# GpSimd takes the low parts of LoRA B, and the third unit runs P7 before P3 with c22 ahead of the tile turns

## The chip, the cores and the metric

The kernel runs on one core of one Trainium2 chip. The metric is the device time of one execution in microseconds. Its engines are TensorE (PE, with its weight loads as PEld), VectorE (DVE), ScalarE (ACT), GpSimd (POOL) and SyncE (SP); each runs its own list of instructions in order, and they wait for one another on semaphores.

## The reference

Two residual layers over 2048 tokens of width 1024 (x has shape 8 x 256 x 1024), all in float32:

```
gate = x @ W_gate.T + 0.5 * (x @ A_gate[i].T) @ B_gate[i].T     # F = 2752, rank 16
up   = x @ W_up.T   + 0.5 * (x @ A_up[i].T)   @ B_up[i].T
act  = silu(gate) * up
x    = x + act @ W_down.T + 0.5 * (act @ A_down[i].T) @ B_down[i].T
x    = x + x @ W.T + bias + scale[j] * (x @ a[j].T) @ b[j].T     # i, j: adapter of the batch entry
```

## The kernel before

Float32 products are made of three matmuls on rounded halves: every operand is split into a high part (a copy rounded to fp32r, made by ScalarE) and a low part (the value less its high part, a subtraction), and high x high, high x low and low x high are summed in PSUM. The tokens are worked through in two halves of 1024. In each half the 2752 rows of gate and up are worked through in 22 units of 128 rows (the last has 64). `U` counts units over both halves (0 to 43), `u` within a half (0 to 21). After both halves come a down stage and an out stage, which the change doesn't touch.

A unit computes a 2 x 2 block of products: gate and up (the two rows) times two chunks of 512 tokens (the two columns): c11, c12 (gate), c21, c22 (up). Units 0 and 1 of a half do this plainly. From unit 2 on, a scheme with seven products in place of eight is used. Its stages are P1 to P7, each of 12 matmuls of 128x512, in an order of its own: P1 P6 P5 P7 P2 D P4 P3 in ordinary units, and in the third unit (u = 2, `PLAIN`) P1 P6 P5 P2 D P3 P7 P4, since some of its inputs are made last. D is one adapter matmul alone; P2, P3 and P4 end in one adapter matmul each. The stages use these weights: P1 A11, P6 S2, P5 S1, P7 S3, P2 A12, P4 A22, P3 S4. A11 to A22 are parts of the turned gate and up tiles (`TG`, `TU`), S1 to S4 sums of them, made by VectorE: s1 = a21 + a22, s2 = s1 - a11, s3 = a11 - a21, s4 = a12 - s2. On the side of the tokens, P1 uses B11, P2 B21, P3 B22, P4 T4, P5 T1, P6 T2, P7 T3, where the T are sums of the x blocks, and T3 and T4 of a half are made and split during units 1 and 2. P3 and P4 are added in PSUM onto earlier contents of their bank, which VectorE must have read before: P3 goes to the bank of P5 (waits for `v_done`), P4 to the bank of P7 (waits for `c22_done`) in the third unit; in ordinary units P4 goes to the bank of P7 and waits for `v_done`, P3 to that of P5 and waits for `c22_done`.

The high and low parts of the weights go through a ring of four slots, in the order of the stages: ScalarE's `w_high` waits until the stage that used the slot four items earlier has ended, then makes the high part; GpSimd's `w_low` (L1839) waits for it and makes the low part; TensorE waits for the low part.

What VectorE does in an ordinary unit, in order: `second_act` of the unit before, `add_q` (L662, after P6), `turn_tile` of G and U of the next unit (L514, which waits for the low parts of A12 and A22 of this unit), in odd units `turn_b`, sums 1 to 3 of the next unit, in eight units of each half (`SPILL_UNITS`, u = 3 to 6 and 9 to 12) a turn of an x block for the spill (`("y", h, n)`, L579), `add_v` (L668 and L670; the first makes `v_done`, both `c22_done`), sum 4, `add_c22` (after D), `b_low`, `first_act` (L695, L698), `add_c12` (L703). In the third unit (`third_unit`): `add_q`, `x_low` of T3, sum 3, `add_v_third` (L677), `x_low` of T4 twice (L614), the turns of G and U, sums 1 and 2, `add_c22_third` (L683, which makes `c22_done`), `add_c22`, sums 3 and 4, `b_low`, `first_act`, `add_c12`.

The adapters: x times LoRA A of a half is in `Tm` (for gate and up), split high and low and stacked over the partitions in bands of 32; `Bf[u % 2]` holds LoRA B in bands that fit: three bands with the high part, one with the low part, for gate (w = 0) and up (w = 1). `ts` holds turned B for two units (`turn_b`, L635). ScalarE's `b_high(U)` (L1471) makes six copies of 32x256, then VectorE's `b_low(U)` (L648) two subtractions of 32x256. An adapter matmul of unit U waits for `bf_lo` at U + 1:

```
            def adapter(U, w, p, dst, start=False):
                h = U // UNITS
                eng.wait_ge(bf_lo, U + 1)
                eng.wait_ge(t_lo, 4 * h + 2 * p + w + 1)
```

In unit 0 of a half `Tm` is only made, so the adapters of unit 0 (E11, E21, E12, E22) run in unit 1, and right behind them E11 and E21 of unit 1 itself. ScalarE makes `b_high` of unit 0, then T1, `Tm`, then `b_high` of unit 1. Every matmul has line L1954 in the profile; operands tell the stages apart: `X_B` are blocks B11, B21, B22, `X_T` are T1, T2, T4 and T3 (also B12, which shares T3's place), `Tm_g,Bf` and `Tm_u,Bf` are adapters.

Of the kernel before, what the change touches and what calls it, by code (L numbers as in the profile page):

```python
# [5 lines left out]
F32 = mybir.dt.float32  # L6
# [32 lines left out]
def build(nc, x, l0_index, l1_index, w_gate, w_up, w_down, a_gate, b_gate, a_up, b_up, a_down, b_down,  # L39
# [19 lines left out]
    with ExitStack() as ctx:  # L59
# [148 lines left out]
        def stages_of(u):  # L208
# [4 lines left out]
            if u == PLAIN:  # L213
                return ["P1", "P6", "P5", "P2", "D", "P3", "P7", "P4"]
# [223 lines left out]
        def b_places(u, w, source, to, also):  # L438

            src = ts[source, :].rearrange("p (r f) -> p r f", r=2)  # L440
            homes = [Bf[u % 2][rows, w, :, :] for rows in (to, also)]
            if u < FULL - 1:
                src = src.rearrange("p r (q c i) -> p r q c i", q=NQ, c=2)[:, :, :, u % 2, :]
                homes = [home.rearrange("p r (q i) -> p r q i", q=NQ) for home in homes]
            elif u == FULL - 1:
                src = src[:, :, 0:P]
            else:
                src, homes = src[:, :, P:P + HC], [home[:, :, w * HC:(w + 1) * HC] for home in homes]
            return src, homes[0], homes[1]
# [30 lines left out]
        def _(eng):  # L480
# [160 lines left out]
            def b_low(U):  # L641
                u = U % UNITS
                eng.wait_ge(bf_hi, U + 1)
                for w in range(2):
                    rows = slice(w * Q, (w + 1) * Q)
                    lo = slice(BF_LO[w] * Q, (BF_LO[w] + 1) * Q)
                    src, dst, hi = b_places(u, w, rows, lo, rows)
                    last = V.tensor_tensor(dst, src, hi.bitcast(F32), ALU.subtract)  # L648
                last.then_inc(bf_lo, 1)

# [90 lines left out]
            def first_unit(U):  # L741
# [19 lines left out]
                b_low(U)  # L761
# [4 lines left out]
                b_low(U + 1)  # L766
# [3 lines left out]
            def second_unit(U):  # L770
# [36 lines left out]
            def unit(U):  # L807
# [19 lines left out]
                b_low(U + 1)  # L827
# [529 lines left out]
        def _(eng):  # L1357
# [102 lines left out]
            def b_high(U):  # L1460
                u = U % UNITS
                eng.wait_ge(b_turned, U // UNITS * BLOCKS + u // 2 + 1)
                if U >= 2:
                    wait_stage(eng, *last_stage(U - 2))
                for w in range(2):
                    if u == FULL:
                        A.activation(Bf[u % 2][:, w, :, (1 - w) * HC:(2 - w) * HC], zeros[:, :, :], ACT.Copy)
                    for r in BF_HI[w]:
                        rows = slice(r * Q, (r + 1) * Q)
                        src, home, _ = b_places(u, w, slice(w * Q, (w + 1) * Q), rows, rows)  # L1470
# [51 lines left out]
            def second_unit(U):  # L1522
# [8 lines left out]
                silu_plain(U)  # L1531
                b_high(U + 1)
                w_high(U + 1, "S1")
# [4 lines left out]
            def third_unit(U):  # L1538
                h = U // UNITS
                copy_p1(U)  # L1540
                w_high(U, "S4")
# [3 lines left out]
                w_high(U, "S3")  # L1545
# [267 lines left out]
        def _(eng):  # L1813
# [37 lines left out]
            def first_unit(U):  # L1851
# [12 lines left out]
                for item in ("A11", "A12", "A21", "A22"):  # L1864
                    w_low(U + 1, item)

            def second_unit(U):
                for item in ("A11", "S2", "S1", "A12"):
                    w_low(U + 1, item)

            def third_unit(U):
                for item in ("S4", "S3", "A22"):
                    w_low(U, item)
                for item in ("A11", "S2", "S1", "S3"):
                    w_low(U + 1, item)
# [25 lines left out]
            for U in range(ALL):  # L1901
# [49 lines left out]
        def _(eng):  # L1951
# [160 lines left out]
            def third_unit(U):  # L2112
# [11 lines left out]
                up(U, "D", adapter(U, 1, 1, d, start=True))  # L2124
                eng.wait_ge(v_done, seven_half(U))
# [268 lines left out]
```

## Time and profile before

| | |
|---|---|
| time, median of 3 runs | 1652.75 us (1651.93 to 1652.83) |
| the profiled execution | 1652.34 us, span 1650.3 us |
| mean granted clock of TensorE | 0.998 |
| TensorE busy | 1615.0 us, 98% |
| VectorE, ScalarE, GpSimd busy | 1129.6, 535.8, 653.8 us (68, 32, 40%) |
| the chain that ended last, by engine | 85% TensorE, 5% VectorE |

The span is the time from the first to the last instruction of the core. TensorE is almost never idle, so its few idle stretches and its granted clock are what a change of order can reach. A matmul's printed duration covers its way through the pipeline, so single ones overlap: read the distance from start to start.

### The profile page before, as it was taken

To read this page: it belongs to the slowest core of one execution; us is meant where nothing else is said; L and a number is where in the kernel's file an instruction comes from. 1 tells how busy PE (TensorE), PEld (TensorE's weight loads), DVE (VectorE), ACT (ScalarE), POOL (GpSimd) and SP (SyncE) were. 2 spreads that over 40 slices of the span, in tenths; PEclk is the share of its full clock that TensorE was granted. 3 is DMA by queue.
4 is the path that set the end of the run, shared out by engine and by line. 5 is a ranking of instruction groups with operands and counts; after the bars stand their busy time and mean duration, and the time that the engine had idled before them with its cause. 6 is when DMAs were issued, how large, how long until landed. Compare 5 with 4: busy or idle time off the path is not lost.

```text
span 1650.3 us, 21023 instructions
## 1 busy us (share of the span) xinstructions
PE 1615.0 (98%) x7060; PEld 1314.0 (80%) x7060; DVE 1129.6 (68%) x1286; ACT 535.8 (32%) x925; POOL 653.8 (40%) x441
## 2 busy tenths in 40 slices
PE   6999999999999899999999999999999999999998
PEld 4778888888887788888888788888888887778886
DVE  5887777777768877777776665566665578856433
ACT  3744444444446444444444221111111121431110
POOL 5254444444452444444444452323332331541110
PEclk9999999999999999999999999999999999999999
DMA  8334434423433344344334742122222131013322
GB/s 158 104 91 109 144 93 106 150 80 96 120 101 91 93 105 144 98 112 146 81 80 128 275 124 67 45 77 80 80 55 77 62 70 28 18 29 80 79 52 53
DMA packets 218125, 156.12 MB, mean 95 GB/s; under 512 B 110692, under 2 KB 200164, under 8 KB 215268
## 3 DMA queue, kind: packets, MB, share of 16 engines
q1 hardware_dynamic: 169536, 114.92, 27.3%
q10 hardware_dynamic: 48356, 39.86, 7.7%
q8 instruction: 58, 0.95, 0.2%
q14 instruction: 47, 0.39, 0.1%
q0 software_dynamic: 128, 0.00, 0.0%
HBM read 115.38 MB, written 39.32 MB: 94 GB/s over the span
## 4 chain that ended last, share of the span: by engine, by line
PE 85%; DVE 5%; SPq 4%; issue 2%; ACT 2%; POOL 1%; DMA 1%; DVEq 0%; ACTq 0%
PE ps L1954 85%; SPq L463 1%; SPq L1207 1%; DVE X_T L614 1%; SPq L1199 1%; ACT Bf L1471 1%; SPq L1171 1%; DVE TU L514 0%; DVE TG L514 0%; POOL W L1839 0%; SPq L1224 0%; DMA raw<-in_L_cond_W_up_dram 0%; DMA act_scratch<-vbuf 0%; DVE s L547 0%; DVE s L540 0%
## 5 line engine op out<-in xcount | busy, mean ns | idle before, releaser
L1954 PE MATMUL ps<-X_T,W 128*128 128x512 f32 x1944 | 460.4, 392 | 11.8 <-DVE vbuf L683 5.2
L1954 PE MATMUL ps<-act,Wd 128*128 128x512 f32 x2016 | 462.4, 390 | 1.4 <-POOL Wd L1888 1.4
L1954 PEld LDWEIGHTS ps<-act,Wd 128*128 128x128 f32 x2016 | 378.6, 188 | 81.5 <-POOL Wd L1888 1.8
L1954 PEld LDWEIGHTS ps<-X_T,W 128*128 128x128 f32 x1944 | 364.7, 188 | 94.2 <-DVE vbuf L668 7.6
L1954 PE MATMUL ps<-X_B,W 128*128 128x512 f32 x1728 | 417.7, 392 | 14.0 <-ACT X_B L1416 13.3
L1954 PEld LDWEIGHTS ps<-X_B,W 128*128 128x128 f32 x1728 | 325.6, 189 | 83.9 <-issue 15.5
L940 DVE TENSOR_TENSOR acc<-acc,ps 128x1024 f32<-128x1024 f32 x176 | 214.1, 1220 | 176.1 <-PE ps L1954 175.6
L1839 POOL TENSOR_TENSOR W<-s,W 128x512 fp32r<-128x512 f32 x156 | 210.8, 1351 | 256.3 <-ACT W L1387 256.3
L1839 POOL TENSOR_TENSOR W<-TG,W 128x512 fp32r<-128x512 f32 x88 | 129.8, 1476 | 175.8 <-ACT W L1387 175.7
L1387 ACT ACTIVATE W<-s 128x512 fp32r<-128x512 f32 x156 | 98.4, 632 | 239.2 <-PE ps L1954 232.7
L1880 POOL TENSOR_TENSOR act<-stage,act 128x1024 fp32r<-128x1024 f32 x42 | 100.6, 2414 | 173.7 <-ACT act L1623 173.7
L1954 PE MATMUL ps<-X1hi,Wo 128*128 128x512 f32 x512 | 141.4, 390 | 0.0
L1954 PEld LDWEIGHTS ps<-X1hi,Wo 128*128 128x128 f32 x512 | 96.2, 188 | 20.4
L1471 ACT ACTIVATE Bf<-ts 32x256 fp32r<-32x256 f32 (+1 forms) x264 | 107.9, 409 | 8.7 <-DVE ts L635 6.1
L1623 ACT ACTIVATE act<-stage 128x1024 fp32r<-128x1024 f32 x42 | 42.4, 1048 | 184.7 <-PE ps L1954 164.8
L662 DVE TENSOR_TENSOR qbuf<-p1buf,ps 128x512 f32<-128x512 f32 x38 | 26.1, 687 | 100.1 <-PE ps L1954 100.0
L1888 POOL TENSOR_TENSOR Wd<-turned,Wd 128x512 fp32r<-128x512 f32 x44 | 55.8, 1291 | 74.0 <-ACT Wd L1657 74.0
L1387 ACT ACTIVATE W<-TG 128x512 fp32r<-128x512 f32 x88 | 55.3, 629 | 91.3 <-PE ps L1954 84.1
L1839 POOL TENSOR_TENSOR W<-TU,W 128x512 fp32r<-128x512 f32 x46 | 65.7, 1431 | 39.4 <-ACT W L1387 39.4
L1954 PE MATMUL ps<-X1lo,Wo 128*128 128x512 f32 x256 | 80.3, 390 | 0.0
L1888 POOL TENSOR_TENSOR Wo<-turned,Wo 128x512 fp32r<-128x512 f32 x16 | 21.7, 1378 | 124.4 <-ACT Wo L1657 124.4
L698 DVE TENSOR_TENSOR c21buf<-c21buf,s1buf 128x512 f32<-128x512 f32 x38 | 67.9, 1787 | 1.3
(134 smaller groups left out, 1512.2 us busy)
## 6 DMA issues: line engine op xcount, KB each, us to landing
stage<-act_scratch SPq DMA_DIRECT2D x21, 1024.0 KB, 5.0
raw<-in_L_cond_W_gate_dram SPq DMA_DIRECT2D x164, 128.0 KB, 3.0
raw<-in_L_cond_W_up_dram SPq DMA_DIRECT2D x164, 128.0 KB, 3.1
raw<-in_x_dram SPq DMA_DIRECT2D x104, 128.0 KB, 3.1
raw<-in_L_cond_W_down_dram SPq DMA_DIRECT2D x88, 128.0 KB, 3.2
act_scratch<-c21buf ACTq DMA_DIRECT2D x42, 256.0 KB, 2.4
act_scratch<-vbuf ACTq DMA_DIRECT2D x42, 256.0 KB, 2.8
xt_scratch<-xt ACTq DMA_DIRECT2D x4, 2048.0 KB, 7.0
```

The lines of the kernel that those rows point to most:

```text
L463: eng.dma_start(buf[q * Q + b * R:q * Q + (b + 1) * R, w * HQ:(w + 1) * HQ], rows[:, q * HQ:(q + 1) * HQ]).then_inc(filled, 16)
L614: V.tensor_tensor(x_home(name, kq, 1), x_source(name, kq), x_home(name, kq, 0).bitcast(F32), ALU.subtract).then_inc(x_lo_d.up((h, name, kq ...
L662: V.tensor_tensor(qbuf[:, :], p1buf[:, :], bank(U % 2, "b"), ALU.add).then_inc(q_done, 1)
L698: V.tensor_tensor(c21buf[:, :], c21buf[:, :], s1buf[:, :], ALU.mult).then_inc(act1_done, 1)
L940: V.tensor_tensor(acc[pr][:, k, :], acc[pr][:, k, :], src[:, :], ALU.add).then_inc(b_added.up(s), 1)
L1387: A.activation(hi, src, ACT.Copy).then_inc(w_hi, 1)
L1471: last = A.activation(home, src, ACT.Copy)
L1623: A.activation(acts[t % 3][:, 0, cols], stage[t % 2][:, cols], ACT.Copy).then_inc(act_hi.up((t, pr)), 1)
L1839: G.tensor_tensor(low, src, hi.bitcast(F32), ALU.subtract).then_inc(w_lo, 1)
L1880: G.tensor_tensor(acts[t % 3][:, 1, cols], stage[t % 2][:, cols], acts[t % 3][:, 0, cols].bitcast(F32), ALU.subtract).then_inc(act_lo.up(( ...
L1888: last = G.tensor_tensor(low, src, hi.bitcast(F32), ALU.subtract)
L1954: return nc.tensor.matmul(dst, stationary, moving, start=start, stop=stop, skip_group_check=True)
```

## The change

Three edits at once. (1) In the third unit P7 moves ahead of P3. S3 and S4 change places in all queues: VectorE makes sum 3 during unit 1 and sum 4 in the third unit. `add_c22_third` and `add_c22` move ahead of the turns and sums of the next unit. On ScalarE S1's high part of the third unit moves ahead of `b_high`. (2) The low parts of LoRA B move from VectorE to GpSimd (`b_low`), placed behind A11's low part of the next unit in most units. ScalarE makes one more copy per unit, a rounded copy of both bands into `b_round`, from which GpSimd subtracts; the bands of `Bf` are arranged so that the low part stands in the band of its source. `b_high` waits until the previous `b_low` has read `b_round`. (3) In the eight spill units `add_v` comes ahead of the turn of the x block.

```diff
-                return ["P1", "P6", "P5", "P2", "D", "P3", "P7", "P4"]
+                return ["P1", "P6", "P5", "P2", "D", "P7", "P3", "P4"]
...
-        TM_LO = (slice(2 * Q, 3 * Q), slice(Q, 2 * Q))
-        TM_AGAIN = (slice(3 * Q, 4 * Q), slice(0, Q))
-        BF_HI = ((0, 1, 2), (1, 2, 3))
-        BF_LO = (3, 0)
+        TM_LO = (slice(2 * Q, 3 * Q), slice(0, Q))
+        TM_AGAIN = (slice(3 * Q, 4 * Q), slice(Q, 2 * Q))
+        BF_HI = ((1, 2, 3), (0, 2, 3))
+        b_round = at("b_round", 209664, [2 * Q, 256], F32R)
...
 VectorE: b_low(U) and every call of it removed
 VectorE, first_unit
                 x_sum(h, "T1", 1)
-                b_low(U)
                 x_low(h, "T2", 0)
...
-                b_low(U + 1)
                 x_low(h, "T1", 1)
 VectorE, second_unit
-                sums(U + 1, (4,))
+                sums(U + 1, (3,))
                 plain_act2(U)
-                b_low(U + 1)
                 x_low(h, "T3", 0)
 VectorE, third_unit
                 x_low(h, "T3", 1)
-                sums(U, (3,))
+                sums(U, (4,))
                 add_v_third(U)
                 x_low(h, "T4", 0)
                 x_low(h, "T4", 1)
+                add_c22_third(U)
+                add_c22(U)
                 turn_tile(("G", U + 1))
                 turn_tile(("U", U + 1))
                 sums(U + 1, (1, 2))
-                add_c22_third(U)
-                add_c22(U)
                 sums(U + 1, (3, 4))
-                b_low(U + 1)
 VectorE, unit
+                add_v(U)
                 if u in SPILL_UNITS:
                     turn_x(("y", h, SPILL_UNITS.index(u)))
-                add_v(U)
                 if u + 1 < FULL:
                     sums(U + 1, (4,))
                 add_c22(U)
-                b_low(U + 1)
 ScalarE, b_high
+                both = slice(0, 2 * Q)
+                if U >= 1:
+                    eng.wait_ge(bf_lo, U)
+                A.activation(b_rounded(u, both), b_places(u, 0, both, both)[0], ACT.Copy)
 ScalarE, second_unit
+                w_high(U + 1, "S1")
                 b_high(U + 1)
-                w_high(U + 1, "S1")
 ScalarE, third_unit
-                w_high(U, "S4")
+                w_high(U, "S3")
                 store_act(U - 1)
                 x_high(h, "T4", 0)
                 x_high(h, "T4", 1)
-                w_high(U, "S3")
+                w_high(U, "S4")
 GpSimd
+            def b_low(U):
+                u = U % UNITS
+                eng.wait_ge(bf_hi, U + 1)
+                eng.wait_ge(w_lo, made[0])
+                for w in range(2):
+                    rows = slice(w * Q, (w + 1) * Q)
+                    src, dst = b_places(u, w, rows, rows)
+                    last = G.tensor_tensor(dst, src, b_rounded(u, rows).bitcast(F32), ALU.subtract)
+                last.then_inc(bf_lo, 1)
+                eng.wait_ge(bf_lo, U + 1)
 GpSimd, first_unit: b_low(U) and b_low(U + 1) behind the four w_low of U + 1
 GpSimd, second_unit
+                w_low(U + 1, "A11")
+                w_low(U + 1, "S2")
+                w_low(U + 1, "S1")
+                b_low(U + 1)
+                w_low(U + 1, "A12")
 GpSimd, third_unit and ordinary units (there A12, A22, S4 first)
+                for item in ("S3", "S4", "A22"):
+                    w_low(U, item)
+                w_low(U + 1, "A11")
+                b_low(U + 1)
+                for item in ("S2", "S1", "S3"):
+                    w_low(U + 1, item)
 TensorE, third_unit
+                eng.wait_ge(q_done, seven_half(U))
+                up(U, "P7", stage_p(U, "P7", b))
                 eng.wait_ge(v_done, seven_half(U))
                 stage_p(U, "P3", c, start=False)
                 up(U, "P3", adapter(U, 0, 1, c))
-                eng.wait_ge(q_done, seven_half(U))
-                up(U, "P7", stage_p(U, "P7", b))
                 eng.wait_ge(c22_done, seven(U))
```

## Rows read from the trace of the kernel before

**Rows 1.** The page, its head and the busy time of the engines.

```profile
span 1650.3 us, 21023 instructions
...
PE 1615.0 (98%) x7060; PEld 1314.0 (80%) x7060; DVE 1129.6 (68%) x1286; ACT 535.8 (32%) x925; POOL 653.8 (40%) x441
```

**Rows 2.** Waits: who waited for whom: us in total, times, longest.

```profile
POOL W L1839 <- ACT W L1387: 471.5, 275, 14.9
...
PEld ps L1954 <- DVE vbuf L668: 7.6, 16, 2.2
...
PE ps L1954 <- DVE vbuf L683: 5.2, 2, 2.6
...
PE ps L1954 <- DVE vbuf L668: 2.2, 2, 1.8
```

**Rows 3.** Timeline of TensorE, units 2 and 3: start, length, [idle before].

```profile
72.26 2.88 PE L1954 MATMUL ps<-X_B,W 128*128 128x512 f32 x12
74.98 2.88 PE L1954 MATMUL ps<-X_T,W 128*128 128x512 f32 x12
78.96 3.00 PE L1954 MATMUL ps<-X_T,W 128*128 128x512 f32 x12 [1.10 <-issue]
...
93.99 4.56 PE L1954 MATMUL ps<-X_T,W 128*128 128x512 f32 x12 [2.57 <-DVE vbuf L683]
...
98.62 2.89 PE L1954 MATMUL ps<-X_B,W 128*128 128x512 f32 x12
...
112.75 3.02 PE L1954 MATMUL ps<-X_T,W 128*128 128x512 f32 x12
```

**Rows 4.** A window: busy time of each engine, then the granted clock.

```profile
93.99:95.00 1.01, 1.01 (x2) 0.83 (x3) 0.96 (x2) 0.59 (x2) 0.86 (x1) 0.50 0.13 35
```

**Rows 5.** Timeline of TensorE in half 1, units 24 and 25.

```profile
524.18 2.88 PE L1954 MATMUL ps<-X_B,W 128*128 128x512 f32 x12
...
531.34 3.01 PE L1954 MATMUL ps<-X_T,W 128*128 128x512 f32 x12 [1.55 <-POOL W L1839]
...
546.12 3.06 PE L1954 MATMUL ps<-X_T,W 128*128 128x512 f32 x12 [2.62 <-DVE vbuf L683]
...
549.24 2.88 PE L1954 MATMUL ps<-X_B,W 128*128 128x512 f32 x12
...
565.25 3.01 PE L1954 MATMUL ps<-X_T,W 128*128 128x512 f32 x12 [1.80 <-DVE vbuf L668]
```

**Rows 6.** Timeline of the other engines, units 2 and 3.

```profile
74.29 2.56 ACT L1471 ACTIVATE Bf<-ts 32x256 fp32r<-32x256 f32 x6 [3.06 <-DVE ts L635]
...
77.59 1.27 POOL L1839 TENSOR_TENSOR W<-s,W 128x512 fp32r<-128x512 f32 x1 [5.47 <-ACT W L1387]
...
85.28 3.44 DVE L614 TENSOR_TENSOR X_T<-xt,X_T 128x1024 fp32r<-128x1024 f32 x2
...
88.65 1.23 DVE L514 STREAM_TRANSPOSE TG<-raw 128x1024 f32<-128x1024 f32 x1
...
93.25 0.68 DVE L683 TENSOR_TENSOR vbuf<-vbuf,ps 128x512 f32<-128x512 f32 x1
...
105.10 1.25 DVE L514 STREAM_TRANSPOSE TG<-raw 128x1024 f32<-128x1024 f32 x1
```

**Rows 7.** Timeline around the first adapters, unit 1 of half 0.

```profile
56.68 2.56 ACT L1471 ACTIVATE Bf<-ts 32x256 fp32r<-32x256 f32 x6
...
59.27 0.85 DVE L648 TENSOR_TENSOR Bf<-ts,Bf 32x256 fp32r<-32x256 f32 x2 [1.90 <-ACT Bf L1471]
...
60.48 0.39 PE L1954 MATMUL ps<-Tm_g,Bf 128*128 128x512 f32 x1
```

**Rows 8.** Groups by line and form: busy, mean ns of one, idle before.

```profile
L1893 POOL TENSOR_TENSOR Ad<-Ad_turned,Ad 128x256 fp32r<-128x256 f32 x11 | 8.2, 747 | 51.0 <-ACT Ad L1680 51.0
```

**Rows 9.** Timeline of VectorE in unit 25, half 1.

```profile
556.89 1.25 DVE L514 STREAM_TRANSPOSE TG<-raw 128x1024 f32<-128x1024 f32 x1 [0.96 <-POOL W L1839]
```

**Rows 10.** The instructions of line L698: duration in ns, min/median/max.

```profile
L698 DVE TENSOR_TENSOR c21buf<-c21buf,s1buf x38: 691/1825/1830, 99.5 to 909.8; 128x512 f32<-128x512 f32 x38
```

More of the change, by code:

```diff
@@ L436, in item_places, with b_places @@
             return src[:, :].rearrange("p (k m) -> p k m", k=KT)[:, ks, :], wo[:, 0, ks, :], wo[:, 1, ks, :]
-        def b_places(u, w, source, to, also):
-            src = ts[source, :].rearrange("p (r f) -> p r f", r=2)
-            homes = [Bf[u % 2][rows, w, :, :] for rows in (to, also)]
+        def b_places(u, w, source, to):
+            src, home = ts[source, :].rearrange("p (r f) -> p r f", r=2), Bf[u % 2][to, w, :, :]
             if u < FULL - 1:
                 src = src.rearrange("p r (q c i) -> p r q c i", q=NQ, c=2)[:, :, :, u % 2, :]
-                homes = [home.rearrange("p r (q i) -> p r q i", q=NQ) for home in homes]
+                home = home.rearrange("p r (q i) -> p r q i", q=NQ)
             elif u == FULL - 1:
@@ L447, in b_places, with b_rounded @@
             else:
-                src, homes = src[:, :, P:P + HC], [home[:, :, w * HC:(w + 1) * HC] for home in homes]
-            return src, homes[0], homes[1]
+                src, home = src[:, :, P:P + HC], home[:, :, w * HC:(w + 1) * HC]
+            return src, home
+        def b_rounded(u, rows):
+            if u < FULL - 1:
+                return b_round[rows, :].rearrange("p (r q i) -> p r q i", r=2, q=NQ)
+            if u == FULL - 1:
+                return b_round[rows, :].rearrange("p (r f) -> p r f", r=2)
+            return b_round[rows, 0:2 * HC].rearrange("p (r f) -> p r f", r=2)
         def load_first(eng, kind, w):
@@ L639, in turn_b @@
                 last.then_inc(b_turned, 1)
[L641 to L649, printed above, removed]
             def t_low(h, p, w):
@@ L1865, in first_unit, with third_unit @@
                     w_low(U + 1, item)
+                b_low(U)
+                b_low(U + 1)
             def second_unit(U):
-                for item in ("A11", "S2", "S1", "A12"):
-                    w_low(U + 1, item)
[L1871 to L1875, printed above, removed]
+                w_low(U + 1, "A11")
[3 more added lines that the diff above has]
+                w_low(U + 1, "A12")
+            def third_unit(U):
+                for item in ("S3", "S4", "A22"):
+                    w_low(U, item)
+                w_low(U + 1, "A11")
+                b_low(U + 1)
+                for item in ("S2", "S1", "S3"):
+                    w_low(U + 1, item)
+            def b_low(U):
[8 more added lines that the diff above has]
+                eng.wait_ge(bf_lo, U + 1)
             def act_low(t, pr):
@@ L1911, in _ @@
                         w_low(U, item)
-                    for item in ("A11", "S2", "S1", "S3"):
+                    w_low(U + 1, "A11")
+                    b_low(U + 1)
+                    for item in ("S2", "S1", "S3"):
                         w_low(U + 1, item)
@@ L1916, in _ @@
                         w_low(U, item)
-                    for item in ("A11", "N", "A12", "S"):
+                    w_low(U + 1, "A11")
+                    b_low(U + 1)
+                    for item in ("N", "A12", "S"):
                         w_low(U + 1, item)
```

3 lines of the change are left out of this document (1 added, 2 removed).

## The prediction

> **What bounds the kernel now.** I read the page first. TensorE is busy for 1615.0 of 1650.3 us; no other engine comes to 70% [rows 1]. So only stretches in which TensorE stands still, or runs at the lower clock, can be won. The profiled execution took 1652.34 us, 2.04 more than its span and 0.41 under the median of 1652.75; the sum below is a difference, and I take it off the median.
>
> Next, the waits of TensorE [rows 2]. The start apart, the largest is 5.2 us in two pieces behind L683, the addition that makes c22 in the third unit of each half. Then comes L668, `v_done`: 2.2 us in two pieces, and, on the weight-load side, 16 waits with 7.6 us. There are 16 units that turn an x block ("y") for the spill.
>
> Then TensorE's timeline through the third unit (unit 2) of half 0 [rows 3]. One stage of 12 matmuls advances the start by 2.72 us (72.26 to 74.98) and one adapter matmul by 0.23. Seven stages and four adapters are 19.95. Unit 2 starts at 72.26 and unit 3 at 98.62, which is 26.36: 6.4 us are lost. P5 starts at 78.96 in place of 77.70, 1.26 late. P4 starts at 93.99 after 2.57 of idle, and its 12 matmuls last 4.56 in place of 2.88. The reader should see two costs in that one row: the wait, and 1.7 us because the granted clock is 0.50, so 1.2 GHz, right behind it [rows 4]. The other 0.9 are restarts and small waits. In half 1 [rows 5] the same unit takes 25.06 (524.18 to 549.24), 5.1 over, with no slow P4.
>
> Last, who is late in that unit [rows 6]. P5 waits for the low part of S1: ScalarE makes six Bf copies from 74.29 for 2.56 us, only then S1's high part, and GpSimd ends the low part at 78.86. P4 waits for c22: VectorE turns G and U of the next unit from 88.65 and makes two sums before L683 at 93.25.
>
> **The change, part by part.** *Order and turns of the third unit.* P7 goes ahead of P3, and both c22 additions ahead of the turns. P7 ends, P3 and its adapter run 2.95, and only then does P4 want c22. L683 needs 0.68 [rows 6] and each hand-over 0.1 to 0.3 (GpSimd ends at 78.86, P5 starts at 78.96), so it has about 2 us to spare. S3 and S4 change places in all queues with it: S3's sum is now made in the unit before, and S4's sum (once for once) is behind `add_q`. Does that hold? Unit 2 now starts at 73.46 (below), so P5 ends at 81.6 and VectorE has made `v_done` by about 83.1. Then the two low parts of T4 on VectorE and those of S4 and A22 on GpSimd take turns, as now (3.44 us for the first two [rows 6]): four of some 1.25, S4's there near 85.6 where P3 wants it at 87.5, A22's near 88.1 to 88.9 where P4 wants it at 90.5. So P4's wait goes, and with it its slow clock.
>
> *S1 ahead of `b_high`.* S1's high part no longer sits behind the Bf copies. Its ring slot frees when d1 of unit 1 ends, one stage and one adapter (2.95) before P1 of unit 2, so it is ready before P5. P5's wait goes. A12 is next behind the Bf copies. These become seven: 7 x 0.42 = 3.0 us. VectorE turns b some 2 us earlier, since unit 1 loses its last `b_low` and the wait in front of it, so they end at about 75.3; two x copies (2.0) and A12 follow, its low part is there near 79.5 to 80, and P2 wants it at 81.6. Covered. Both halves' third units therefore run at about 19.95: 6.4 + 5.1 = 11.5 us are removed, before what is added.
>
> *`b_low` on GpSimd.* It removes two VectorE operations per unit (0.42 each [rows 7]) and adds one ScalarE copy (0.42) and two GpSimd subtractions. No row has 32x256 on GpSimd. From below: VectorE's 0.42 each. From above: 1.27 for 128x512 [rows 6]. The nearest row is 128x256 at 0.75 [rows 8], the same elements in each partition, so I take 1.5 for the pair and keep 0.85 to 2.6.
> In ordinary units this is hidden. After P7 ends, ScalarE makes A11 and seven copies (0.2 + 0.6 + 3.0), GpSimd the pair and then S2's low part: about 0.5 + 1.5 + 1.3, so it is there after some 7.4 us. P6 of the next unit wants it 4 stages and 4 adapters later, 11.8 us. 4.4 are to spare. GpSimd idles 471.5 us behind ScalarE's high parts [rows 2].
> It isn't hidden at the adapters of unit 1. There ScalarE starts the copies of unit 1 at 56.68, ends them 2.56 later, VectorE's pair ends at 60.12, and TensorE takes that adapter at 60.48 without a wait [rows 7]. Now there is one more copy in each of `b_high(U)` and `b_high(U+1)`, 0.85 later: 60.1. The pair ends at 61.6, so E11 of unit 1 starts about 1.2 late. The same rows stand in half 1. Added: 2 x 1.2 = 2.4 us.
>
> *What is late next: unit 3.* The turns have not become cheaper, only later. With unit 1's loss, unit 2 starts at 73.46, P7 ends at 87.5 and unit 3 starts at 93.4. VectorE takes c22 at 87.75, and does then the work it did from 88.65 on. From the turn of G(3) to that of G(4) it was 16.45 us (88.65 to 105.10 [rows 6]), which hangs on the chain L703, silu, `copy_p1`, A12's high and low part. Less 0.85 for the moved `b_low`, and some 0.3 of a wait for P4 in it, it is 15.3. So G(4) is turned from 103.05, and from there to P4 of unit 3 it was 7.65 (105.10 to 112.75) in half 0 and 8.36 (556.89 to 565.25) in half 1 [rows 3, 5, 6, 9]. Without the x turn (1.2), that is now behind `add_v`, 6.45 and 7.2: P4 of unit 3 at 109.5 to 110.25. I take 110.0. Its ideal would be 107.5, so 2.5 us are given back. A second path says nearly the same: S2's low part now waits for `b_low`, which waits for seven copies behind G(3)'s turn; it comes at about 98, P6 wants it at 96.1.
> Before, P4 of unit 3 stood at 112.75: half 0 wins 2.75. In half 1 everything lies 451.92 later (524.18 less 72.26), P4 at 561.9 against 565.25: 3.35.
> GpSimd and VectorE are a cost in this. L698 with both inputs in SBUF takes 0.69 at least and 1.83 in most units [rows 10], there with a GpSimd operation under way. I count one such wait for S4's sum and one for L698. The Trainium skill (SBUF — State Buffer, section on the two separate sides) has a rule that speaks against moving `b_low` there: a VectorE operation with two SBUF inputs and a GpSimd operation lock each other out for a whole instruction. By the rule both waits stand; if the two ran side by side, each half would win about 0.7 more, 1.4 in all.
>
> *The x turn behind `add_v` in the other 14 spill units.* There P4 starts 0.06 late and lasts 0.14 longer (3.02 against 2.88, as at 112.75 [rows 3]): 0.2. One is 0.7 (idle 0.42, the smaller of the two in rows 2). VectorE's x turn takes as long as its other turns (1.23 to 1.25), and the lateness is less in each: 13 x 0.2 + 0.7 = 3.3 us won. Its raw slot frees 1.3 us later; the load that takes it is wanted in the next unit, some 15 us on.
>
> **Sum:** 2.75 + 3.35 + 3.3 = 9.4 us off: 1643.3 us. The down and out stages are untouched.
>
> **Rivals.** *Given back little.* If VectorE's chain is some 2 us shorter per half than I make it (fewer waits between it and GpSimd), unit 3 runs near its ideal: 4 to 5 us more, 1639. For it: the operations alone are shorter than in the trace. Against: the chain is the trace's own, measured.
> *The clock falls elsewhere.* Half 0's idle 2.57 brought 0.50 [rows 4]; half 1's 2.62, 1.55 and 1.80 did not (12 matmuls in 3.01 to 3.06 behind each [rows 5]). The new waits (E11, P6 and P4 of unit 3, each 1 to 2 us) could bring it in two places: 2 x 1.7, 1646.7. The Trainium skill (TensorE: Matmul & The Clock Gate, Part 1) says that idleness brings the lower clock and that it needs busy time to rise again; by that the new waits are suspects, and the rule gives no more than this rival has.
> *Given back whole.* G(4), and with it `v_done`, comes 2 to 3 us later per half (b copies, turn and A12 in an unlucky order), or the 14 small waits stay: 3 to 6 us less, 1647 to 1650; at its end no change that can be told.
> *Slower: the pair on GpSimd is long.* Each half pays for it twice, at E11 and in front of S2 or in the chain to G(4). With a pair of X us the loss is 4 (X - 1.5): nothing is won from X = 3.9, and it is slower by over 0.2% from X = 4.7, 2.35 us an operation. Beyond 5.9 the ordinary units' slack goes too, each of some 36 paying the rest. At X = 5.5: 16 lost, 1659. For it: strided reads of 32 partitions have no row. Against: 1.27 for twice the elements.
>
> **Chances and range.** A measurement can tell about 0.2%, 3.3 us, from no change: faster is under 1649.4. Forecast (1641 to 1646) 0.62; given back little 0.13; clock 0.09; given back whole 0.10, of which 0.06 within 0.2%; slower 0.05; the last 0.01 lies with no change. So faster 0.88, same 0.07, slower 0.05. The range leaves out the slow end and the luckiest: 1638.5 to 1648.
>
> **What would show it.** Right: P5 and P4 of the third units start without idle and P4 lasts 2.9; new idle of about 1.2 at the first `Tm_g,Bf` of unit 1 behind POOL Bf; P6 or P4 of unit 3 late by 2 to 3 in all; no weight-load waits behind L668 in units 4 and on; POOL Bf pairs of about 1.5, ScalarE Bf copies 7 a unit, POOL busy up by about 60 us. Wrong: P4 of the third units behind POOL W or X_T; a pair over 2.6; P6 waits in ordinary units; granted clock 0.50 behind E11 or in unit 3.

## The result, and the profile after

The changed kernel takes 1642.49 us (median of 5 runs, 1641.36 to 1645.11) against 1652.37 for the kernel before (median of 5 beside it, 1651.93 to 1652.83): ratio 0.9939 [0.9927, 0.9951], so 9.9 us faster. The forecast was 1643.3. The profiled execution took 1642.49 us, 1.69 more than its span. Unchanged code has new line numbers: L1971 is the matmul (L1954 before), L680 c22's addition in the third unit (L683), L665 `v_done` (L668), L1834 `w_low` (L1839), L521 and L586 the turns of weights and of x (L514, L579), L1466 the Bf copies (L1471). New are L1460, the rounded copy of `b_high`, and L1886, `b_low` on GpSimd.

The page of after, its head, the engines, and the group of the new pair (busy time, mean ns of one, idle before):

```profile
span 1640.8 us, 21154 instructions
...
PE 1609.4 (98%) x7060; PEld 1313.4 (80%) x7060; DVE 1069.9 (65%) x1198; ACT 554.2 (34%) x969; POOL 727.0 (44%) x529
...
L1886 POOL TENSOR_TENSOR Bf<-ts,b_round 32x256 fp32r<-32x256 f32 (+1 forms) x88 | 73.4, 834 | 64.7 <-ACT Bf L1466 45.7
```

Against [rows 1] VectorE has 59.7 us less, GpSimd 73.2 more, TensorE 5.6 less. The waits of TensorE in after (total, times, longest):

```profile
PE ps L1971 <- POOL W L1834: 3.8, 2, 1.9
PE ps L1971 <- POOL Bf L1886: 2.6, 2, 1.6
```

All of TensorE's waits that [rows 2] named are gone: the two pieces behind c22, the waits behind `v_done`, the 16 on the weight-load side. Two new pairs stand in their place. TensorE's timeline of after shows where (start, length, idle before): the first adapters of unit 1, then units 2 and 3 of half 0, then half 1.

```profile
60.30 0.39 PE L1971 MATMUL ps<-Tm_u,Bf 128*128 128x512 f32 x1
62.30 0.50 PE L1971 MATMUL ps<-Tm_g,Bf 128*128 128x512 f32 x1 [1.62 <-POOL Bf L1886]
...
74.22 2.88 PE L1971 MATMUL ps<-X_B,W 128*128 128x512 f32 x12
76.94 5.60 PE L1971 MATMUL ps<-X_T,W 128*128 128x512 f32 x24
...
94.17 2.88 PE L1971 MATMUL ps<-X_B,W 128*128 128x512 f32 x12
98.93 8.40 PE L1971 MATMUL ps<-X_T,W 128*128 128x512 f32 x36 [1.88 <-POOL W L1834]
...
110.35 1.98 PE L1971 MATMUL ps<-X_T,W 128*128 128x512 f32 x8
...
507.01 0.39 PE L1971 MATMUL ps<-Tm_g,Bf 128*128 128x512 f32 x1
...
509.03 0.50 PE L1971 MATMUL ps<-Tm_g,Bf 128*128 128x512 f32 x1 [0.94 <-POOL Bf L1886]
...
520.97 2.88 PE L1971 MATMUL ps<-X_B,W 128*128 128x512 f32 x12
...
540.91 2.88 PE L1971 MATMUL ps<-X_B,W 128*128 128x512 f32 x12
545.67 8.41 PE L1971 MATMUL ps<-X_T,W 128*128 128x512 f32 x36 [1.88 <-POOL W L1834]
...
557.09 2.88 PE L1971 MATMUL ps<-X_T,W 128*128 128x512 f32 x12
```

The third unit (P1 at 74.22 to the next P1 at 94.17) takes 19.95 us, and 19.94 in half 1; it was 26.36 and 25.06 [rows 3, 5]. P5 follows P6 within one row, P4 lasts as long as its neighbours. E11 of unit 1 is late: 62.30 where 60.53 would follow, 1.77, and in half 1 509.03 where 507.92 would (four adapters of 0.23 from 507.01), 1.11. P6 of unit 3 is late by 98.93 - 94.17 - 2.72 = 2.04 in both halves. P4 of unit 3 has no wait; it stands at 110.35 where it stood at 112.75, and at 557.09 where it stood at 565.25. (The row at 110.35 is cut by the view's edge.)

The other engines of after in the same stretch show what these two waits hang on:

```profile
58.06 2.56 ACT L1466 ACTIVATE Bf<-ts 32x256 fp32r<-32x256 f32 x6
60.75 1.50 POOL L1886 TENSOR_TENSOR Bf<-ts,b_round 32x256 fp32r<-32x256 f32 x2 [8.02 <-issue]
...
88.47 0.69 DVE L680 TENSOR_TENSOR vbuf<-vbuf,ps 128x512 f32<-128x512 f32 x1 [1.72 <-PE ps L1971]
89.87 1.24 DVE L521 STREAM_TRANSPOSE TG<-raw 128x1024 f32<-128x1024 f32 x1
...
92.15 2.55 ACT L1466 ACTIVATE Bf<-ts 32x256 fp32r<-32x256 f32 x6
...
94.78 2.15 POOL L1886 TENSOR_TENSOR Bf<-ts,b_round 32x256 fp32r<-32x256 f32 x2 [1.57 <-ACT Bf L1466]
97.01 4.73 POOL L1834 TENSOR_TENSOR W<-s,W 128x512 fp32r<-128x512 f32 x3
...
103.07 1.25 DVE L521 STREAM_TRANSPOSE TG<-raw 128x1024 f32<-128x1024 f32 x1 [0.35 <-POOL W L1834]
```

Copies, pair, adapter stand in a row at 58.06, 60.75, 62.30. In unit 2 GpSimd waits 1.57 for the copies, makes the pair in 2.15, and only at 97.01 begins S2's low part, for which P6 has been waiting since 96.9. G(4) is turned at 103.07.

### The profile page after: what moved, and what is told of

It reads as the page before. It is cut to its first block, busy times and chain, and to the rows that moved or that the text cites. A ratio compares the mean times of both kernels' runs of the same rounds, so it can differ in the third digit from the quotient of the medians.

```text
span 1640.8 us, 21154 instructions
## 1 busy us (share of the span) xinstructions
PE 1609.4 (98%) x7060; PEld 1313.4 (80%) x7060; DVE 1069.9 (65%) x1198; ACT 554.2 (34%) x969; POOL 727.0 (44%) x529
## 4 chain that ended last, share of the span: by engine, by line
PE 91%; SPq 3%; issue 2%; DVE 2%; ACT 1%; DMA 1%; POOL 1%; DVEq 0%; ACTq 0%
PE ps L1971 91%; SPq L1199 1%; DMA Ad_raw<-in_L_cond_A_down_dram 1%; ACT Bf L1466 1%; SPq L1285 1%; POOL Bf L1886 0%; SPq L470 0%; DVE acc L932 0%; DVE tw_down L940 0%; SPq L1216 0%; SPq L1191 0%; POOL W L1834 0%; SPq L1267 0%; DVE Ad_turned L899 0%; SPq L1163 0%
## 5 line engine op out<-in xcount | busy, mean ns | idle before, releaser
L1971 PE MATMUL ps<-act,Wd 128*128 128x512 f32 x2016 | 462.5, 389 | 1.6 <-POOL Wd L1901 1.5
L1971 PE MATMUL ps<-X_T,W 128*128 128x512 f32 x1944 | 455.9, 389 | 5.0 <-POOL W L1834 3.8
L1971 PEld LDWEIGHTS ps<-act,Wd 128*128 128x128 f32 x2016 | 378.3, 188 | 82.0 <-POOL Wd L1901 1.8
L1971 PE MATMUL ps<-X_B,W 128*128 128x512 f32 x1728 | 417.4, 391 | 14.3 <-ACT X_B L1408 13.5
L1971 PEld LDWEIGHTS ps<-X_T,W 128*128 128x128 f32 x1944 | 364.7, 188 | 81.8 <-issue 6.2
L1971 PEld LDWEIGHTS ps<-X_B,W 128*128 128x128 f32 x1728 | 325.8, 189 | 83.4 <-issue 14.9
L1834 POOL TENSOR_TENSOR W<-s,W 128x512 fp32r<-128x512 f32 x156 | 211.6, 1358 | 133.0 <-ACT W L1379 130.1
L1834 POOL TENSOR_TENSOR W<-TG,W 128x512 fp32r<-128x512 f32 x88 | 128.9, 1466 | 150.4 <-ACT W L1379 150.1
L1971 PE MATMUL ps<-X1hi,Wo 128*128 128x512 f32 x512 | 141.4, 390 | 0.0
L1971 PEld LDWEIGHTS ps<-X1hi,Wo 128*128 128x128 f32 x512 | 96.1, 188 | 20.6
L1466 ACT ACTIVATE Bf<-ts 32x256 fp32r<-32x256 f32 (+1 forms) x264 | 108.5, 411 | 3.1
L1886 POOL TENSOR_TENSOR Bf<-ts,b_round 32x256 fp32r<-32x256 f32 (+1 forms) x88 | 73.4, 834 | 64.7 <-ACT Bf L1466 45.7
L1834 POOL TENSOR_TENSOR W<-TU,W 128x512 fp32r<-128x512 f32 x46 | 65.7, 1431 | 39.3 <-ACT W L1379 39.3
L1971 PE MATMUL ps<-X1lo,Wo 128*128 128x512 f32 x256 | 80.3, 390 | 0.0
```

The lines of the kernel that those rows point to most:

```text
L1466: last = A.activation(home, src, ACT.Copy)
L1834: G.tensor_tensor(low, src, hi.bitcast(F32), ALU.subtract).then_inc(w_lo, 1)
L1886: last = G.tensor_tensor(dst, src, b_rounded(u, rows).bitcast(F32), ALU.subtract)
L1971: return nc.tensor.matmul(dst, stationary, moving, start=start, stop=stop, skip_group_check=True)
```

## The experiments

Each kernel has 4 to 8 timed runs, beside 9 to 13 of the kernel before on the same chip. Times are medians; ratios are to those runs of the kernel before (medians of 1652.53 to 1653.49 us).

**y_ahead**: the changed kernel with the x turn ahead of `add_v` again.

```
-                add_v(U)
                 if u in SPILL_UNITS:
                     turn_x(("y", h, SPILL_UNITS.index(u)))
+                add_v(U)
```

> The changed kernel, with the x turn of the spill units back ahead of `add_v` (the third edit undone). My theory: the 16 small waits behind the first addition of `add_v` were the x turn alone, 3.3 us by the gaps of the trace before, some 0.2 in each unit, and they come back: about 3 us slower than the changed kernel, 1645.5. Rival: VectorE has lost `b_low` and has room now, so the order no longer matters: within 0.5 us of the changed kernel, 1642.5.

1646.93 us, 0.9964 [0.9951, 0.9977], 4.4 over the changed kernel. The 16 waits are back (weight-load side: total, times, longest), and in this execution the clock fell behind P6's wait in unit 3 (a window: busy time of each engine, then the granted clock):

```profile
PEld ps L1971 <- DVE vbuf L665: 5.5, 16, 0.5
```

```profile
100.00:101.00 1.00, 1.00 (x4) 0.81 (x3) 0.12 (x1) 0.00 (x0) 1.00 (x1) 0.50 0.03 12
```

The spans differ by 4.2. 16 x 0.2 for the waits and 1.6 for the clock (the row of P6, P5 and P7 lasts 10.02 in place of 8.40) are 4.8, and E11's waits are 0.7 shorter here (1.9 against 2.6): 4.1. The term of the x turn holds.

**y_behind_alone**: that edit alone on the kernel before (the same two lines the other way round).

> The kernel before, with the third edit alone (x turn of the spill units behind `add_v`). My theory: the 16 weight-load waits behind the first addition of `add_v` go: 14 x 0.2 + 0.7, and 1.2 of the 2.1 us in unit 25, where the x turn is 1.2 of what VectorE is late by: 4 to 5 us faster than before, 1648. The waits for c22 and P5 in the third units stay. Rival: a VectorE operation behind it (sum 4, `b_low`, c22) becomes late in its turn: 1651 or more.

1648.59 us, 0.9972 [0.9962, 0.9983]: 4.1 us off, as expected. Here the clock was full behind half 0's c22 wait, and fell behind half 1's, the reverse of [rows 4, 5]:

```profile
545.00:549.00 4.00, 4.00 (x12) 3.15 (x13) 3.96 (x5) 0.39 (x1) 2.91 (x2) 0.63 0.09 23
```

**low_behind_s1**: the changed kernel with the third unit's `b_low` behind S2 and S1 on GpSimd.

```
-                w_low(U + 1, "A11")
-                b_low(U + 1)
-                for item in ("S2", "S1", "S3"):
+                for item in ("A11", "S2", "S1"):
                     w_low(U + 1, item)
+                b_low(U + 1)
+                w_low(U + 1, "S3")
```

> The changed kernel, with GpSimd's `b_low` in the third unit behind the low parts of A11, S2 and S1 (in place of behind A11). My theory: the 1.88 us for which P6 of unit 3 waits in each half is the pair on GpSimd in front of S2's low part, and it goes; but the x2 later step, P4 of unit 3, then waits some 0.9 us for `v_done`, since the turn of G waits for A12's low part, which GpSimd reaches no earlier. Net 1.0 us a half, 2 in all: 1640.5. Rival 1: nothing is given back, 3.9 us faster than the changed kernel, 1638.6. Rival 2: S2's low part is late because ScalarE's seven copies are, and the pair's place is worth nothing: 1642.5.

1641.74 us, 0.9933 [0.992, 0.9947]: no more than 0.8 off the changed kernel. P6's wait is gone, and P4 of unit 3 waits for `v_done` in its place, 2.03 after 0.9 expected:

```profile
PE ps L1971 <- DVE vbuf L665: 4.1, 2, 2.0
```

```profile
109.70 3.04 PE L1971 MATMUL ps<-X_T,W 128*128 128x512 f32 x12 [2.03 <-DVE vbuf L665]
```

P4 moves from 110.35 to 109.70 only, and that is not the edit: E11's wait, ahead of it, is 0.86 here against 1.62. From P1 of unit 2 (73.18) to P4 are 36.52, against 36.13 in the changed kernel (74.22 to 110.35). There were two chains of nearly one length, and one edit takes one away.

**v_ahead**: low_behind_s1, and in unit 3 `add_v` also ahead of sums 1 to 3 of the next unit.

```
+                if u == PLAIN + 1:
+                    add_v(U)
                     sums(U + 1, (1, 2, 3))
...
-                add_v(U)
+                if u != PLAIN + 1:
+                    add_v(U)
```

> The changed kernel with `b_low` of GpSimd behind S1's low part in the third unit (as in the earlier run of that edit alone, which moved the wait from P6 to P4 of unit 3), and in unit 3 alone also `add_v` ahead of sums 1 to 3. My theory: the wait of 2.0 us at P4 of unit 3 is only the order of VectorE's work (`v_done` stands behind three sums); it goes but for some 0.2. Faster than the changed kernel by 3.5 us, 1638.5. Rival 1: P7 or the turns set it, `v_done` comes no earlier: 1641.5. Rival 2: the sums become late for S2 of unit 4: a new wait of 1 us or more at P6 of unit 4, 1640.5.

1638.05 us, 0.9914 [0.99, 0.9927]. No wait behind L665 is left. Both chains are gone, and 4.4 us with them. From P1 of unit 2 to P4 of unit 3 are 34.28 (73.25 to 107.53), 1.85 less than in the changed kernel, and as much in half 1: 3.7 us. In this execution E11's waits are shorter too, 1.4 against 2.6.

**three_covered**: v_ahead, and in unit 1 the adapters E11 and E21 moved behind the next chunk of matmuls.

```
-                return ["first", "E11", "E21", "c1", "c", "E12", "d1", "d", "E22"]
+                return ["first", "c1", "c", "E11", "E21", "E12", "d1", "d", "E22"]
...
-                up(U, "E11", adapter(U, 0, 0, a))
-                up(U, "E21", adapter(U, 1, 0, b))
...
+                up(U, "E11", adapter(U, 0, 0, a))
+                up(U, "E21", adapter(U, 1, 0, b))
```

> As the run with `add_v` ahead in unit 3, and in unit 1 of each half E11 and E21 behind the stages c1 and c (so that 5.4 us lie between the adapters of unit 0 and those of unit 1). My theory: the waits at E11 (1.8 and 1.1 in the changed kernel) go, since GpSimd's pair ends 1 to 2 us late, not 5. Silu of unit 1 comes later on ScalarE, in front of S2's high part, which has some 3 us to spare. 2.5 us faster than without it, 1636. Rival: the high parts of S2, S1 and A12 come later with the silu, and P6 or P2 of unit 2 waits by 1 us or more: no gain over the run without it, 1638.5.

1634.91 us, 0.9891 [0.9876, 0.9906]: the fastest kernel of the study, 7.6 under the changed one, in four runs from 1634.69 to 1635.61. TensorE's timeline, P1 of unit 2, then P6 of unit 3, has neither of the new waits: between them lie 22.85 us, and eight stages of 2.72 and four adapters of 0.23 are 22.68.

```profile
72.08 2.88 PE L1974 MATMUL ps<-X_B,W 128*128 128x512 f32 x12
...
94.93 8.41 PE L1974 MATMUL ps<-X_T,W 128*128 128x512 f32 x36
```

**low_twice**: the changed kernel with GpSimd's pair made twice in units 4 to 21 of each half.

```
+                if u > PLAIN + 1:
+                    for w in range(2):
+                        rows = slice(w * Q, (w + 1) * Q)
+                        src, dst = b_places(u, w, rows, rows)
+                        last = G.tensor_tensor(dst, src, b_rounded(u, rows).bitcast(F32), ALU.subtract)
```

> The changed kernel, with the pair of `b_low` made twice on GpSimd in units 4 and on of each half (units 4 to 21, 18 units a half; the result is the same). My theory: in ordinary units the pair is hidden, with 4.4 us to spare and 1.5 to 2.2 for the second pair: no change within 1 us, 1642.5. Rival: the second pair pushes S2's low part or A12's into the path, or locks VectorE out of its additions: 36 x 0.3 or more, 1653.

1642.25 us, 0.9935 [0.9922, 0.9949], the changed kernel's time. The group of the extra operations on the page:

```profile
L1888 POOL TENSOR_TENSOR Bf<-ts,b_round 32x256 fp32r<-32x256 f32 (+1 forms) x72 | 57.1, 793 | 44.6 <-ACT Bf L1466 42.5
```

57.1 us more of work on GpSimd cost nothing: of the 4.4 us of slack forecast for an ordinary unit at least the 1.6 of a second pair are there.

**low_on_vector**: the changed kernel with the pair back on VectorE in its old places, reading the rounded copy.

```
-                    last = G.tensor_tensor(dst, src, b_rounded(u, rows).bitcast(F32), ALU.subtract)
+                    last = V.tensor_tensor(dst, src, b_rounded(u, rows).bitcast(F32), ALU.subtract)
```

> The changed kernel, with the pair of subtractions back on VectorE in its old places, but still from the rounded copy (seven ScalarE copies). My theory: the move to GpSimd is not what wins. The wait at E11 of unit 1 shrinks by the 0.65 us by which VectorE's pair is shorter (1.5 against 0.85), in each half; P6 of unit 3 waits 0.5 to 1.5 in place of 1.9; P4 of unit 3 begins to wait for `v_done` by up to 0.85. Sum within 2 us of the changed kernel, 1641.5. Rival: VectorE needs the relief, the late turns of unit 3 make `v_done` late by 1.5 to 2.5 us a half: 1645 or more.

1648.0 us, 0.997 [0.9959, 0.9982]. My theory was wrong by 6.5 us; the rival's side stood. The waits of TensorE:

```profile
PE ps L1968 <- DVE vbuf L674: 3.7, 2, 1.9
PE ps L1968 <- issue: 2.2, 2, 1.2
...
PE ps L1968 <- DVE Bf L654: 1.4, 2, 1.0
PE ps L1968 <- POOL W L1848: 0.8, 2, 0.4
PE ps L1968 <- DVE qbuf L668: 0.7, 2, 0.4
```

L674 is `v_done`: P4 of unit 3 waits 1.9 in each half. The two pieces without a releaser are at P2 of unit 2. In half 1 of this execution the clock fell behind the wait for `v_done` (the 12 matmuls last 4.61), so about 1.6 of the 6.5 us are the clock:

```profile
560.80 4.61 PE L1968 MATMUL ps<-X_T,W 128*128 128x512 f32 x12 [1.87 <-DVE vbuf L674]
```

**order_and_y**: the kernel before with edits (1) and (3), without (2).

```
-                return ["P1", "P6", "P5", "P2", "D", "P3", "P7", "P4"]
+                return ["P1", "P6", "P5", "P2", "D", "P7", "P3", "P4"]
...
+                add_c22_third(U)
+                add_c22(U)
                 turn_tile(("G", U + 1))
```

> The kernel before with the first and the third edit alone: new order of the third unit, x turn behind `add_v`; `b_low` stays on VectorE with the old layout and six copies. My theory: nearly all of the gain lies in these two. No wait at E11 of unit 1 (1.8 and 1.1 in the changed kernel); against that P2 of unit 2 waits 0 to 0.8 for A12, since the b turn and the copies come 2 us later, and P4 of unit 3 0 to 1.5 for `v_done`. 1641.5, between 1639.5 and 1643.5. Rival: joined with the old `b_low`, the order loses most of its gain, since VectorE's chain through units 2 and 3 is 1.7 us longer: 1646 or more.

1646.57 us, 0.9959 [0.9946, 0.9972]: a miss again, and for the same reason. The waits:

```profile
PE ps L1954 <- DVE vbuf L668: 3.8, 2, 1.9
PE ps L1954 <- issue: 2.4, 2, 1.2
...
PE ps L1954 <- DVE qbuf L662: 0.8, 2, 0.4
PE ps L1954 <- POOL W L1839: 0.8, 2, 0.4
```

**order_y_v_ahead**: order_and_y, with `add_v` ahead of sums 1 to 3 in unit 3 as in v_ahead.

```
+                if u == PLAIN + 1:
+                    add_v(U)
```

> The kernel before with the first and third edit, `b_low` on VectorE in the old layout, and in unit 3 `add_v` ahead of sums 1 to 3. My theory: the move of `b_low` was needed because `v_done` stands behind three sums in unit 3, where VectorE is late; with `add_v` ahead the 1.9 us at P4 of unit 3 go in each half, and what stays is 1.4 at P2 of unit 2, 0.5 at P6 and 0.7 at P7 of unit 3: 4 us faster than without `add_v` ahead (1646.6), 1642.5, as fast as the changed kernel. Rival: VectorE is late in the whole of unit 3, and its `b_low` puts the wait on P3 or on the next unit: 1645.

1641.1 us, 0.9927 [0.9914, 0.9941], 5.5 under order_and_y by the medians. Its two waits for `v_done` (3.8) are gone. Those of P2 of unit 2 are down from 2.4 to 1.3, but that belongs to the execution: part of unit 0 ran at 1.2 GHz in it, so TensorE reached unit 2 of half 0 at 74.22, in place of 72.45, and P2 had nothing to wait for there.

**low_alone**: the kernel before with edit (2) alone, in the old order.

```
-            def b_low(U):
-                u = U % UNITS
...
-                b_low(U + 1)
                 first_act(U)
```

> The kernel before, with the second edit alone (`b_low` on GpSimd with the rounded copy; old order of the third unit, x turn ahead of `add_v`). My theory: alone it is worth nothing to speak of. It costs the waits at E11 of unit 1 (1.1 to 1.8 in each half) and gives back about as much, since the b copies come 2 us earlier and P5 of the third unit no longer waits (1.3 and 1.7 before); the wait for c22 (2.6 a half) and the 16 small waits stay, of the wait in unit 25 one us goes. 1651.5, within 1.5 us of before. Rival: relief of VectorE is itself what wins, as the slower run with `b_low` on VectorE might suggest: 1648 or less.

1644.16 us, 0.9946 [0.9933, 0.996], where I expected 1651.5: the largest miss of the study. VectorE's timeline around unit 1's turn of b, first of the kernel before and then of low_alone:

```profile
61.48 1.23 DVE L610 TENSOR_TENSOR xs<-xt,xs 128x1024 f32<-128x1024 f32 x1
...
65.12 1.38 DVE L540 TENSOR_TENSOR s<-TU 128x512 f32<-128x512 f32 x1
...
73.12 1.14 DVE L635 STREAM_TRANSPOSE ts<-raw 64x256 f32<-64x256 f32 x2
```

```profile
59.44 1.23 DVE L617 TENSOR_TENSOR xs<-xt,xs 128x1024 f32<-128x1024 f32 x1
...
63.08 0.69 DVE L547 TENSOR_TENSOR s<-TU 128x512 f32<-128x512 f32 x1
...
70.24 1.17 DVE L642 STREAM_TRANSPOSE ts<-raw 64x256 f32<-64x256 f32 x2
```

The same operations stand 2.04 earlier at the x sum and 2.88 earlier at the turn of b. So the Bf copies and S1's high part behind them come earlier too, and P5's wait is gone with no edit to the order. The wait for c22 is 0.78 in place of 2.57, and 1.06 in place of 2.62 in half 1 (timelines of VectorE and TensorE in low_alone, half 0):

```profile
92.78 0.69 DVE L680 TENSOR_TENSOR vbuf<-vbuf,ps 128x512 f32<-128x512 f32 x1 [0.17 <-PE ps L1971]
...
93.53 3.01 PE L1971 MATMUL ps<-X_T,W 128*128 128x512 f32 x12 [0.78 <-DVE vbuf L680]
```

The 0.78 overstates what VectorE gained. Its addition stands only 0.47 earlier than before (93.25 [rows 6]), since TensorE itself is late in half 0 of this execution: E11 waits 1.97, and behind that wait the clock fell for another 1.6 (low_and_y, below, is free of that fall):

```profile
63.00:64.00 1.00, 1.00 (x4) 0.81 (x3) 0.82 (x2) 0.86 (x1) 0.00 (x0) 0.50 0.84 275
```

**low_and_y**: edits (2) and (3) in the old order, that is the changed kernel with edit (1) undone.

```
-                return ["P1", "P6", "P5", "P2", "D", "P7", "P3", "P4"]
+                return ["P1", "P6", "P5", "P2", "D", "P3", "P7", "P4"]
...
-                add_c22_third(U)
-                add_c22(U)
                 turn_tile(("G", U + 1))
                 turn_tile(("U", U + 1))
                 sums(U + 1, (1, 2))
+                add_c22_third(U)
+                add_c22(U)
```

> The changed kernel with the first edit undone (old order P3, P7, P4, turns ahead of the c22 additions, S1 behind the b copies); `b_low` on GpSimd and the x turn behind `add_v` stay. My theory now: the edits overlap. With `b_low` away from VectorE the wait for P5 is gone and that for c22 is down to 0.8 and 1.1 (as in the run of that edit alone), and the early turns of the old order let unit 3 start with no wait at P6, where the new order waits 1.9 twice. So the new order is worth nothing in this company: the run of `b_low` alone (1644.2) less 3.3 for the small waits: 1641, between 1639.5 and 1642.5, not slower than the changed kernel. Rival: the order still carries its part, as I first forecast: 1645 or more.

1639.83 us, 0.9921 [0.9908, 0.9935]: not slower than the changed kernel, and 2.7 faster by the medians (the intervals overlap). TensorE's timeline:

```profile
73.78 2.88 PE L1971 MATMUL ps<-X_B,W 128*128 128x512 f32 x12
...
92.00 3.04 PE L1971 MATMUL ps<-X_T,W 128*128 128x512 f32 x12 [1.06 <-DVE vbuf L680]
...
95.11 2.88 PE L1971 MATMUL ps<-X_B,W 128*128 128x512 f32 x12
97.83 1.52 PE L1971 MATMUL ps<-X_T,W 128*128 128x512 f32 x6
```

And c22's addition on VectorE:

```profile
91.27 0.68 DVE L680 TENSOR_TENSOR vbuf<-vbuf,ps 128x512 f32<-128x512 f32 x1
```

The third unit takes 21.33, 1.38 more than in the changed kernel, and then P6 of unit 3 follows at once, where the changed kernel waits 2.04. c22's addition stands 1.98 earlier than in the kernel before (93.25), with the turns still ahead of it: that is what VectorE gains when `b_low` leaves it.

**low_y_late**: low_and_y with E11 and E21 moved as in three_covered.

```
-                return ["first", "E11", "E21", "c1", "c", "E12", "d1", "d", "E22"]
+                return ["first", "c1", "c", "E11", "E21", "E12", "d1", "d", "E22"]
```

> As the run without the first edit, with E11 and E21 of unit 1 behind the stages c1 and c. Its waits of 2.1 and 0.7 us at E11 go: 2.5 us faster than that run, 1638.5. With the new order, `b_low` behind S1 and `add_v` ahead in unit 3 it was 1634.9; if both theories hold, the new order pays 2.5 to 4 us once its own waits are covered. Rival: the silu that comes later delays S1, which stands behind the b copies in the old order, and P5 waits again: 1641.

1639.28 us, 0.9916 [0.9903, 0.993]: 0.6 under low_and_y, where I had put the waits that go at 2.5. E11's waits go, but P2 of unit 2 now waits in half 0 and c22's waits grow from 2.1 to 2.5:

```profile
PE ps L1971 <- DVE vbuf L680: 2.5, 2, 1.4
...
PE ps L1971 <- issue: 1.0, 1, 1.0
```

## Why the prediction was right, and where it was wrong

The sum came out: 9.4 us forecast, 9.9 measured, 9.85 between the two profiled executions. So did most of its terms.

*Order and turns of the third unit; S1 ahead of `b_high`.* Both third units were forecast at 19.95 and measure 19.95 and 19.94. The 11.5 us are gone.

*`b_low` on GpSimd.* The pair was put at 1.5 and takes 1.50 undisturbed (60.75); over all units the mean is 1.67, so GpSimd's busy time rose by 73 us and not by about 60. Ordinary units hide it: no wait there, and low_twice doubled it for nothing. At E11 2 x 1.2 were forecast; 1.77 and 1.11 were measured, 2.9. In half 0 the six copies began at 58.06, where two more copies of 0.42 would put them at 57.52; the rest is that lateness of 0.54. The step was right. Its size in half 0 belongs to the execution: six other kernels have the same code up to that adapter, and TensorE idled there for 0.86 (low_behind_s1), 1.04 (y_ahead), 1.15 (v_ahead), 1.31 (low_and_y), 1.75 (low_twice) and 1.97 (low_alone), against 1.62 in the changed kernel. Why it varies stays open.

*What is late next: unit 3.* G(4) was forecast at 103.05 and stood at 103.07, P4 of unit 3 at 110.0 and stood at 110.35. The first hit is luck in part: c22's addition came 0.72 later than forecast (88.47 against 87.75), and the work from there to G(4) took 14.60 in place of 15.3. The size of the term was right, but the binding link was the other one. It was named as the second path: S2's low part behind `b_low`, which "comes at about 98, P6 wants it at 96.1", so 1.9 late; measured 2.04. `v_done` did not bind in the changed kernel; low_behind_s1 showed that it stands right behind (P4 at 109.70). Half 0 won 2.4 (2.75 forecast). Up to P4 of unit 25 565.25 - 557.09 = 8.16 are won, of which 4.48 stand already at the first adapter of unit 23 (507.01, in the kernel before 511.49): half 1 won 3.7 (3.35 forecast).

*The x turn behind `add_v`.* Forecast 3.3. The spans differ by 9.5; less 2.4 and 3.7 that leaves 3.4, and y_ahead and y_behind_alone confirm it from both sides.

*The lock.* The prediction counted on waits between GpSimd and VectorE. The pair took 2.15 at 94.78, beside VectorE's sums, which read two inputs in SBUF. It took 1.50 at 60.75, beside turns, and 1.51 in low_and_y, beside additions that read PSUM. The Trainium skill (SBUF — State Buffer, section on the two separate sides) has the two engines lock each other out, as the prediction told, and these rows agree. No run took the lock away, so its whole price stays open.

**What was wrong is whom the sum credited.** The step "`b_low` on GpSimd" booked edit (2) as a cost of 2.4, with 0.85 per half given back in the chain to G(4); the rest of its gain sat, uncounted, in "VectorE turns b some 2 us earlier" under the step on S1, and the 11.5 us were credited to the order and to S1's place. The runs show the reverse: edit (2) alone brings 8.4 us, edit (3) alone 4.1, edits (1) and (3) together 6.2, edits (2) and (3) together 13.7, all three 9.9. Edit (1) alone wasn't run. Edits (2) and (3) add up (12.5 singly, 13.7 together); edit (1) adds 2.1 to edit (3), but nothing to (2) and (3), since it and edit (2) cure the same waits. That it is the engine, and not the rounded copy or the new bands, low_on_vector shows: it differs from the changed kernel in the engine of the pair alone, and is 5.5 us slower (about 1.6 of it the clock). VectorE's chain through unit 1 is shorter by two operations and by the idle in front of them (1.90 [rows 7]), and that alone removes P5's wait and brings c22's addition 1.98 earlier (low_and_y), which takes c22's wait from 2.6 to 1.1. What edit (1) then still has to win is 1.38 us per half. It pays 2.04 for it at P6: with c22 ahead of the turns, G(3) is turned at 89.87, in place of 86.65 in low_and_y, and everything on the way to S2's low part follows. That is 0.66 a half, 1.3 in all. E11's waits, 2.6 against 1.8, bring it to 2.1 of the 2.8 us between the two profiled executions (1642.49 and 1639.66); but the part of half 0 has the same code ahead of it in both, so it isn't the order's. The last 0.7 wasn't traced. So in the change as it stands the new order is worth nothing, and may cost up to 2.7. With GpSimd, VectorE and the early adapters in the order of three_covered, the kernel is 1639.28 - 1634.91 = 4.4 faster than low_y_late, the old order with the adapters moved. That compares two arrangements, and is not the price of edit (1) by itself: low_y_late lacks the moves of `b_low` and of `add_v`. In its trace P6 and P4 of unit 3 don't wait, and these are the waits that the two moves cure, so they should win little there; no run joins them with the old order.

*The clock.* The prediction took the 1.7 us of P4 at 0.50 as removed. Half-rate stretches stood behind c22 in half 0 (before), behind c22 in half 1 (y_behind_alone), behind E11 (low_alone), behind P6 of unit 3 (y_ahead) and behind `v_done` in half 1 (low_on_vector); behind the four new waits of the changed kernel there is none in its profile. So this term belongs to an execution, and a change can only remove waits behind which it may fall. Whether the run of the changed kernel that took 1645.11 had one stays open; it has no trace, only a mean granted clock of 0.997, against 0.999 in the profiled execution, and a run of 1643.02 shows the same 0.997.

## What to carry to other kernels

Before three edits are booked one by one, ask of each what it would do alone: two cures for one wait don't add, and the side effect on a busy engine's queue (two small operations and the idle ahead of them) can be worth more than the edit meant for the wait. Where the next chain is nearly as long as the one removed, find the third as well; here moving `b_low` on GpSimd alone brought 0.8 us, with VectorE's order 4.4, and with the early adapters 7.6. A wait that varies by a microsecond between executions of the same code, as E11's did, has to be set aside before two profiles are compared. An engine's slack in ordinary units says nothing of the two places per half where its result is wanted at once.

## What the runs showed of the hardware

A 32x256 subtraction on GpSimd takes 0.75 us, as much as the 128x256 of [rows 8]: a quarter of the partitions made it no shorter. It is 1.8 times VectorE's 0.42, and was 1.08 beside VectorE's sums (2.15 for the pair); over all 88 operations of the changed kernel the mean is 0.83.

Idle stretches of TensorE of 1.9 to 2.6 us brought the granted clock from 2.4 to 1.2 GHz in some places of some executions and not in others, for a loss of 1.6 to 1.7 us each time. P6's wait of 1.88 did so in y_ahead and in neither half of the changed kernel. c22's wait did so in half 0 of the kernel before and in half 1 of y_behind_alone, and in the other half of neither. In unit 0, behind a wait of 2.0 to 2.2 us for an x block, it fell in six of the profiled executions, and not in four others with such a wait (order_and_y, y_behind_alone, v_ahead, three_covered); in one of the six (order_y_v_ahead) it put all that follows 2 us later.
